# Counts from a summed one-hot tile, two weight loads moved behind the first tables, a residual split moved into the first attention: one layer of a language model on one core

## What is computed

```python
h = rms_norm(rms_norm(emb[x], w) @ proj.T)
att = softmax(where(causal, q @ k.T / 4, -inf)); y = att @ v        # q, k, v from layernorm(h)
h = h + y @ wo
h = h + (silu(layernorm(h) @ w_gate.T) * (layernorm(h) @ w_up.T)) @ w_down.T
```

## Time and profile before

| | us |
|---|---|
| median of 3 runs | 743.83 |
| lowest and highest | 742.55, 744.45 |
| profiled execution, its own time | 744.75 |
| its span, first to last instruction | 743.0 |
| PE busy in it | 701.0 (94%) |
| DVE, ACT, POOL busy | 416.8, 352.2, 295.3 |

### The profile page before, as it was taken

The page is one execution under the profiler, slowest core; times in us unless marked ns, Lnnn a source line. Parts: engine busy times, 40 slices in busy tenths (PEclk is TensorE's granted clock), DMA queues, the critical chain, the costliest instruction groups (busy, mean ns, idle before and its releaser), DMA issues.

```text
span 743.0 us, 16193 instructions
## 1 busy us (share of the span) xinstructions
PE 701.0 (94%) x6301; PEld 529.8 (71%) x6301; DVE 416.8 (56%) x1038; ACT 352.2 (47%) x722; POOL 295.3 (40%) x402
## 2 busy tenths in 40 slices
PE   5819979999899999999999999999999999999998
PEld 2617758996389848985698659964997489857873
DVE  5895578777565546545565456554655465444320
ACT  6775436775256514652266216640665046521320
POOL 5020021323146643654366516753465437530220
PEclk9968999999999999999999999999999999999999
DMA  8948220001100021001100120003000210000000
GB/s 329 393 166 290 101 89 1 2 1 45 45 30 1 2 63 56 2 3 59 60 1 3 45 73 2 3 1 103 16 1 2 78 41 2 3 15 15 1 1 28
DMA packets 10458, 40.35 MB, mean 54 GB/s; under 512 B 1808, under 2 KB 2576, under 8 KB 8592
## 3 DMA queue, kind: packets, MB, share of 16 engines
q1 hardware_dynamic: 6912, 25.44, 8.8%
q0 software_dynamic: 3328, 13.11, 5.7%
q10 hardware_dynamic: 144, 0.79, 0.3%
HBM read 29.89 MB, written 9.44 MB: 53 GB/s over the span
## 4 chain that ended last, share of the span: by engine, by line
PE 85%; DVE 10%; ACT 2%; issue 1%; DMA 1%; DVEq 0%; ACTq 0%
PE banks L1067 14%; PE banks L1069 14%; PE banks L1068 14%; PE banks L1151 6%; PE banks L1153 6%; PE banks L1152 6%; PE banks L1021 4%; PE banks L1039 3%; PE banks L1100 2%; PE banks L1101 2%; PE banks L1102 2%; PE banks L1010 2%; PE banks L1045 1%; PE banks L1046 1%; DMA group_table<-yT_split 1%
## 5 line engine op out<-in xcount | busy, mean ns | idle before, releaser
L1068 PE MATMUL banks<-xnT_and_h,ffn_weights 128*128 128x256 f16 x1024 | 279.7, 273 | 0.0
L1069 PE MATMUL banks<-xnT_and_h,ffn_weights 128*128 128x256 f16 x1024 | 279.7, 273 | 0.0
L1067 PE MATMUL banks<-xnT_and_h,ffn_weights 128*128 128x256 f16 x1024 | 279.6, 273 | 0.1
L365 POOL TENSOR_TENSOR gated_split<-gate_work,gated_split 128x256 f16<-128x256 f32 x128 | 86.5, 676 | 271.5 <-ACT gated_split L512 271.5
L369 POOL TENSOR_TENSOR weights_split<-weights,weights_split 128x512 f16<-128x512 f32 x96 | 111.1, 1157 | 0.0
L1067 PEld LDWEIGHTS banks<-xnT_and_h,ffn_weights 128*128 128x128 f16 x1024 | 101.3, 99 | 12.1 <-DVE xnT_and_h L863 0.6
L1069 PEld LDWEIGHTS banks<-xnT_and_h,ffn_weights 128*128 128x128 f16 x1024 | 100.4, 98 | 11.9
L1068 PEld LDWEIGHTS banks<-xnT_and_h,ffn_weights 128*128 128x128 f16 x1024 | 100.2, 98 | 11.5
L500 ACT ACTIVATE gate_work<-banks,scales 128x256 f32<-128x256 f32 x128 | 60.7, 474 | 99.8 <-PE banks L1069 99.6
L813 DVE SCALAR_TENSOR_TENSOR weights<-weights,counts_T 128x512 f32<-128x512 f32 x128 | 87.7, 685 | 18.5 <-ACT weights L508 18.3
L508 ACT ACTIVATE weights<-banks,scales 128x512 f32<-128x512 f32 x128 | 87.3, 682 | 14.5 <-PE banks L1021 14.5
(11 more groups left out here) (235 smaller groups left out, 1090.2 us busy)
## 6 DMA issues: line engine op xcount, KB each, us to landing
ffn_weights<-in_ffn_w SPq DMA_DIRECT2D x12, 1024.0 KB, 15.2
out_rows_dram<-ffn_weights SPq DMA_DIRECT2D x16, 256.0 KB, 2.0
xnT_and_h<-in_wqkv SPq DMA_DIRECT2D x1, 1536.0 KB, 8.2
local_table<-gated_split SPq DMA_DIRECT2D x2, 640.0 KB, 6.3
local_table<-xnT_and_h SPq DMA_DIRECT2D x2, 640.0 KB, 3.6
gated_split<-in_projT SPq DMA_DIRECT2D x4, 256.0 KB, 3.9
ffn_weights<-in_wo SPq DMA_DIRECT2D x1, 1024.0 KB, 10.2
token_table<-weights_split ACTq DMA_DIRECT2D x1, 768.0 KB, 6.9
```

The lines of the kernel that those rows point to most:

```text
L365: g.tensor_tensor(gtl[:, j, :], g2[j % 2], gth[:, j, :], ALU.subtract).then_inc(gt_lo, 1)
L1067: t.matmul(o, wh, xTh[m % 2][:, c, :], start=c == 0, stop=False)
L1068: t.matmul(o, wh, xTl[m % 2][:, c, :], start=False, stop=False)
L1069: last = t.matmul(o, wl, xTh[m % 2][:, c, :], start=False, stop=c == DC - 1)
```

## The change

- **Counts.** DVE adds the four one-hot tiles of each sequence's first half to one (`t_onsum`, two `tensor_tensor` of 128x512 and 128x256 float16, behind L615's step). PE adds the summed tile once in place of four, so a second half takes five matmuls and not eight. The banks are made in the order 0, 2, 1, 3 and taken out in that order.
- **Pairs 6 and 7** of gate and up are loaded by SP behind the first group table and the landing of the first fetch from it, no longer right behind pair 5. Their four half squares stand on ACT in slots 2 to 5 of phase 0, the matmul `gu_sum` on PE in slot 7 (before: ahead of `turn(0)`).
- **`wo_low`** is cut in two halves of 128x1024 and stands on DVE in slots 5 and 10 of phase 0. SP's wait ahead of pair 11 and PE's ahead of the first `wo` matmuls ask for both halves.

```diff
+COUNT_ORDER = (0, 2, 1, 3)
+SQUARE_SLOTS = {2: (6, 0), 3: (6, 1), 4: (7, 0), 5: (7, 1)}
+GU_SUM_SLOT = 7
+WO_LOW_SLOTS = (5, 10)
+        t_onsum = t_junk[:, 3584:4096].rearrange("p (b t u) -> p b t u", b=B, t=2)
...
-            for i in range(8):
+            for i in range(6):
                 load_pair(i)
             write_local(0)
             write_groups(0)
+            sp.wait_ge(mG_in[0], 16)
+            for i in (6, 7):
+                load_pair(i)
...
-            sp.wait_ge(tab["wo_lo"], 1)
+            sp.wait_ge(tab["wo_lo"], 2)
             load_pair(11)
             write_groups(1)
...
-            for i in range(4):
-                actq.wait_ge(tab["counts"], i + 1)
+            for n, i in enumerate(COUNT_ORDER):
+                actq.wait_ge(tab["counts"], n + 1)
...
-            for i in range(1, 8):
+            for i in range(1, 6):
                 squares(i)
...
                     if n == 0:
+                        if s in SQUARE_SLOTS:
+                            half_squares(*SQUARE_SLOTS[s])
...
+            on4 = t_on.rearrange("p (b t u) -> p b t u", b=B, t=TILES // B)
+            dve.wait_ge(tab["onehot"], 1)
+            link(v.tensor_tensor(t_onsum, on4[:, :, 0:2, :], on4[:, :, 2:4, :], ALU.add))
+            v.tensor_tensor(t_onsum[:, :, 0, :], t_onsum[:, :, 0, :], t_onsum[:, :, 1, :], ALU.add).then_inc(tab["onsum"], 1)
...
-            wo_low()
             scan(1)
...
+                    if n == 0 and s in WO_LOW_SLOTS:
+                        wo_low(WO_LOW_SLOTS.index(s))
...
-            for q in range(4):
+            for q in COUNT_ORDER:
                 b, top = divmod(q, 2)
-                for e in range(4 * (top + 1)):
-                    src = on[:, b * per + e, :]
-                    if e < 4 * top:
-                        last = t.matmul(bank[q], src, t_tri[:, P:P + 512], start=e == 0, stop=False)
...
+                if top:
+                    pe.wait_ge(tab["onsum"], 1)
+                    t.matmul(bank[q], t_onsum[:, b, 0, :], t_tri[:, P:P + 512], start=True, stop=False)
+                for e in range(4):
+                    n = (4 - e) * P
+                    last = t.matmul(bank[q][:, 512 - n:512], on[:, b * per + 4 * top + e, :], t_tri[:, 0:n],
+                                    start=top == 0 and e == 0, stop=e == 3)
...
             pe.wait_ge(tab["scan"], 32)
-            pe.wait_ge(tab["gu_sq"], 16)
-            t.matmul(f_bank[0][:, 0:16], ones32, pm[:, 0:16], start=True, stop=True).then_inc(tab["gu_sum"], 1)
...
+                    if n == 0 and s == GU_SUM_SLOT:
+                        pe.wait_ge(tab["gu_sq"], 16)
+                        t.matmul(f_bank[0][:, 0:16], ones32, pm[:, 0:16], start=True, stop=True).then_inc(tab["gu_sum"], 1)
```

More of the change, by code:

```diff
@@ L209, in lm_block @@
             "key", "perm", "seen_mm", "index", "kn", "kn_ev", "kb", "kb_ev", "qT", "qT_ev", "s_tab", "scan", "groups",
-            "vf", "gu_sq", "gu_sum", "gu_scaled", "gstep", "gram", "dn_diag", "dn_sum", "dn_max", "dn_scaled")}
+            "onsum", "vf", "gu_sq", "gu_sum", "gu_scaled", "gstep", "gram", "dn_diag", "dn_sum", "dn_max", "dn_scaled")}
         tok_out, g_out = sem("token_table_written"), [sem(f"group_table{b}_written") for b in range(2)]
@@ L422, in _, with half_squares, squares @@
             a.activation(e_pcT, bank[5], ACT.Copy).then_inc(tab["pcT_ev"], 1)
-            def squares(i):
+            def half_squares(i, m):
                 actq.wait_ge(ffn_in[i], 16)
                 src = raw_pair(i).rearrange("p (c m n) -> p m c n", c=2, m=2)
[L427 to L432, removed]
+                u = 2 * i + m
+                if u >= 2:
+                    actq.wait_ge(tab["gu_sq"], u - 1)
+                a.activation(t_sq[:, (2 + u % 2) * CH:(3 + u % 2) * CH].rearrange("p (c n) -> p c n", c=2), src[:, m],
+                             ACT.Square, accum_out=pm[:, u:u + 1]).then_inc(tab["gu_sq"], 1)
+            def squares(i):
+                half_squares(i, 0)
+                half_squares(i, 1)
             actq.wait_ge(wo_in, 16)
@@ L711, in group_step, with wo_low @@
                                     ALU.max).then_inc(tab["gstep"] if j < 7 else tab["groups"], 1)
-            def wo_low():
+            def wo_low(i):
                 dve.wait_ge(tab["wo_hi"], 1)
-                v.scalar_tensor_tensor(Wo[:, DC * D:2 * DC * D], t_wo, s_wo, Wo[:, 0:DC * D], ALU.mult,
-                                       ALU.subtract).then_inc(tab["wo_lo"], 1)
+                w = DC * D // 2
+                v.scalar_tensor_tensor(Wo[:, DC * D + i * w:DC * D + (i + 1) * w], t_wo[:, i * w:(i + 1) * w], s_wo,
+                                       Wo[:, i * w:(i + 1) * w], ALU.mult, ALU.subtract).then_inc(tab["wo_lo"], 1)
             def weight_scales():
@@ L904, in _ @@
             per = SEQ // P
-            for q in range(4):
+            for q in COUNT_ORDER:
                 b, top = divmod(q, 2)
-                for e in range(4 * (top + 1)):
-                    src = on[:, b * per + e, :]
-                    if e < 4 * top:
-                        last = t.matmul(bank[q], src, t_tri[:, P:P + 512], start=e == 0, stop=False)
-                    else:
-                        n = (4 * (top + 1) - e) * P
-                        last = t.matmul(bank[q][:, 512 - n:512], src, t_tri[:, 0:n], start=e == 0, stop=e == 4 * top + 3)
+                if top:
[5 more added lines that the diff above has]
+                                    start=top == 0 and e == 0, stop=e == 3)
                 last.then_inc(tab["counts"], 1)
@@ L1096, in phase @@
                             if tl == 0:
-                                pe.wait_ge(tab["wo_lo"], 1)
+                                pe.wait_ge(tab["wo_lo"], 2)
                             for c in range(DC):
```

## The result

The changed kernel takes **747.2 us** (median of 6 runs, 746.33 to 748.42), the kernel before 743.69 in the 6 runs beside it: a ratio of 1.0059, 95% interval 1.0034 to 1.0085. The profiled execution took 747.03 with a span of 745.3.

The account below looks back on a forecast made before the run. PE bounds the kernel from phase 1 on; phase 0 waits for the second group table's write. The early gain of 1.05 us is swallowed; +2.0 for the later copy and +0.6 for the clock give +2.6, median 746.4, range 743.9 to 749.0.

Parts of the forecast that it names:

- Start of phase 0: Phase 0 starts 1.95 us earlier: 1.3 from the counts and 0.65 from moving the split of wo.
- The second scan behind PE's last score: With wo's split (2.26 us) off DVE's path, only 0.65 us is gained; PE's last score is next to limit.
- The counts' 1.3 us: At the start, six fewer 512-column matmuls on PE save 1.3 us; the other end was 2.6.
- so the 1.3 us arrives at the scan: From p to the first scan each engine waits for the one before, so the counts' gain of 1.3 us carries through.
- Squares: ACT's slots in phase 0 run 0.4 us over, 1.5 in all; PE loses 0.7 by slot 6, gu_sum adds 0.2.
- The write: Second group table's write, behind pair 11 on SP, issued at 77.6, lands at 82.4; ACT's yT copy comes 2.0 us later.
- The clock: After PE's longer stall, 4 to 6 us at low clock in place of 3.6 cost 0.6 us more (0.2 to 1.2).
- rival in which the stall goes: Group table lands before ACT needs it; stall and slow matmuls vanish: -5.2 us, 738.6; chance 0.06.
- Sum: Whole kernel: +2.0 for the later copy and +0.6 for the clock, +2.6 us, median 746.4.
- The signs: Profile marks; wrong if ACT idles under 2.4 us, copy before 80.5, second-scan banks late, or phase 1 not 2 to 3 us later.
- The fetches hold phase 0: Late first group fetch or pair 6 delays phase 0 or its squares: +4.6 us, 748.4; chance 0.08.
- The early gain is larger: Counts give up to 2.6 us, squares cost only 0.2; 744.1 to 745.5; chance 0.19 with what lies between.

Follow-up runs that it names:

- e1: Changed kernel with the second group table's write moved on SP ahead of the wait for pair 11: 742.07 us.
- e2: Changed kernel with the second group table written on SP ahead of pairs 8 to 11: 739.04 us, ratio to before 0.9929.
- e4: Kernel before with only the second group table's write moved ahead of pairs 8 to 11: 738.24 us, ratio 0.9925.
- e6: Kernel before with only the split of wo moved to slots 5 and 10: 746.53 us, ratio 1.0047.
- e8: Kernel before, unchanged, run again for a second profile: 743.36 us, ratio 1.0000.
- e3: Changed kernel with 20 more filling matmuls (results unused) in slot 12 of phase 0: 743.51 us.
- e12: Kernel before with nine more filling matmuls (results unused) in slot 12 of phase 0: 740.93 us, ratio 0.9962.
- e11: Changed kernel with the second group table written ahead of pairs 8 to 11, run once more: 737.32 us, ratio to before 0.9914.
- e9: Kernel before with the second group table written ahead of pairs 8 to 11 and the wo split in slots 5 and 10: 738.01 us, ratio 0.9929.
- e10: Kernel before with the group table written first, the wo split in slots 5 and 10 and the summed-tile counts: 738.17 us, ratio 0.9927.
- e7: Kernel before with only the moved pairs 6 and 7, their squares in slots 2 to 5 and the sum in slot 7: 746.88 us, ratio 1.0055.
- e5: Kernel before with only the counts' part (summed tile, bank order), wo_low's halves in a row between the scans: 743.99 us, ratio 1.0004.

## Why the prediction was right, and where it was off

**The mechanism** was the one forecast, and e1, e2, e4 and e6 show it: the wait for the split, moved to slot 10, holds pair 11 and the group table's write behind it on SP. Step by step, against e8:

- *Start of phase 0*: -1.95 forecast, -1.9 in the profiles. But the two halves of it are not equally firm. The second scan behind PE's last score gave 0.6 us as worked out: from the first scan to the second it is 11.6 us before and 11.0 in the changed kernel. **The counts' 1.3 us is the mis-sized term.** PE did reach `p` earlier, at 9.6 to 10.6 us in the seven profiles with the summed tile against 10.7 to 12.1 in the six without it that began at 5.5: 1.4 us on average. The first scan, though, came at 32.3 to 33.9 against 32.4 to 33.8, on average 32.96 and 33.17: 0.2 us, within the spread of single executions. That e8 against the changed kernel shows 1.3 is luck: 0.8 of it is ACT, which came to its first bank at 10.48 in e8, after a wait of 1.42 us for a load, and at 9.65 in the changed kernel. The step that failed is "so the 1.3 us arrives at the scan", because the path changes. In all seven profiles without the summed tile, the first one too, the chain up to 20 us runs over PE; in all seven with it, it runs over ACT's banks of counts and a row of small DVE steps behind them (the chain of the changed kernel):

```profile
12.94 0.49 ACT counts_T L421
13.42 0.59 ACT ffn_weights L422 x2
...
14.10 0.17 DVE token_rows L645
...
20.31 0.24 DVE scales L664
20.55 0.14 issue
20.68 0.35 PE banks L967 x2
```

  I wrote "ACT takes banks out in the new order as they come"; in ACT's timeline they were there before ACT was, and it takes them out with no gap:

```profile
11.74 0.61 ACT L421 ACTIVATE counts_T<-banks 128x512 f16<-128x512 f32 x1
12.22 0.62 ACT L422 ACTIVATE ffn_weights<-banks 128x512 f16<-128x512 f32 x1
...
12.79 0.63 ACT L421 ACTIVATE counts_T<-banks 128x512 f16<-128x512 f32 x1
```

  From ACT's first bank to the first scan it takes 22.9 us in the changed kernel, and 22.9 to 24.0 in the six profiles without the summed tile that began at 5.5 (e8 23.3). So 0 to 1.1 us was to be had there. The profile that I read hid it: with PE late by the stumble the same stretch was 27.1 us.
- *Squares*: 0.4 us over a slot, PE 0.7 later, `gu_sum` 0.2. Measured: first `turn` to slot 10 took 21.1 us against 20.2, 0.9, and the stacks stood 1.9 us apart (59.84, 61.72, 63.59, 65.47). The size is right, though a pair of profiles shows it only roughly: with the squares in the slots this stretch took 20.0 to 21.2 us in six profiles, without them 19.4 to 20.4 in eight.
- *The write*: pair 11 forecast at 77.6 in the time of the first profile, 74.8 with the stumble taken off; it went at 74.7. Landing 4.8 us behind that forecast, 5.3 measured. The copy +2.0 forecast, +1.8 against e8.
- *The clock*: 0.6 us forecast for its extra cost. Against e8, from the copy to the last `wo` matmul it is 8.5 against 8.2, 0.3; but e3 and e12 show the whole cost of the low clock to be 3 to 4 us in either kernel, where I took 1.8 for before. My rival in which the stall goes was priced at -5.2 for the changed kernel; e2 and e11, in which it does go, stand 4.5 and 6.0 us under the runs of before beside them.
- *Sum*: +2.0 in the profiles (e8 to the changed kernel), +3.5 in the medians. With 0.2 in place of 1.3 for the counts my own sum would be +3.7, an estimate close to the medians. The clock is the other candidate. The record has the mean granted clock of every run, over its whole length. The kernel before has 78 such runs in the experiments: 13 at 0.981 or above, with a median of 740.0 us, 24 at 0.979 with 742.7, and 41 at 0.977 or below with 744.4. The six runs of the changed kernel lie at 0.968 to 0.977, and their median is 2.8 us above those 41. So some executions of before keep a higher clock, and none of the changed kernel did; e12, before with PE kept busy, has none under 0.979. The mean doesn't say in which stretch the clock was low, so how the last 1.5 us divide between the two stays open.
- *The signs*: two that I had set for "wrong" came true by the letter, a copy before 80.5 (80.07) and a phase 1 that starts other than 2 to 3 us later (1.5 us against the first profile, 1.8 against e8). Both were set in the time of the first profile, with PE late by 2.8 us; the order of events, the waits and what released them were the forecast ones.

**The rivals.** "The fetches hold phase 0" did not happen in the changed kernel, but does in e9 and e10, without its moved pairs. "The early gain is larger" did not happen. On completion order (the Trainium skill, DMA: Bandwidth & Descriptors, Queues, rings and completion order: taken in order, but not complete in order per issuing engine): where I looked, the write landed about 0.3 us behind the last pair issued before it (first profile of before, the changed kernel, e7), so no overtaking shows here. How long it took follows what was still in the queue: 7.5 to 11.1 us behind four pairs, 8.4 behind three, 4.9 to 5.1 where pair 11 alone was left, and 1.7 in front of all (e2, e4, e9 and e11; 3.0 in e10).

## What to carry to other kernels

Before a wait is moved in an engine's list, name what stands behind it there: here a finished 128 KB write sat behind a load that it had nothing to do with, and putting it first was worth 5 us to the one kernel and 8 to 10 to the other, more than any part of the change. Price a removed piece of work by the engine that is next, in more than one profile, since one late instruction at the start can show slack that isn't there. And where TensorE has to stand still for a microsecond or more, count its slower matmuls afterwards as well as the stall, or give it something to do.

## What the runs showed of the hardware

- DVE's first conversion, 128x16, took 2.62 us in the first profile of the kernel before and 0.32 to 0.59 in the thirteen others; GpSimd's third select, 128x128, started near 3.16 in each, and ran 0.29 us in the first profile and 2.34 in the thirteen others. So in every profile one of the two took 2 us longer at this point. Where it was GpSimd, its select released PE's first matmul at 5.50; where it was DVE, PE began at 8.28. No run tried the cause.
- PE stood still for 0.90 and 1.60 us in the two profiles of before, for 1.76 in e1 and 1.86 in e5, and in each the granted clock was at 1.2 GHz for most of the `wo` matmuls behind it. With filling matmuls in the same place it stood still for 0.44 (e12) and 0.22 us (e3), and the clock stayed at 2.4 GHz. In before the fill gained 3.1 us, more than PE had stood still.
- A write of 128 KB landed 1.7 us after its issue with nothing ahead of it in the queue, and 11.06 us behind four loads of 1 MB (e7).
